# Queries and keys of a head rotated together on GpSimd, and projected three heads ahead

## The chip, the cores and the metric

One core of one Trainium2 chip. The metric is the device time of one execution in microseconds (us), the median of several runs.

## The reference

A token embedding with a layer norm (8 sequences of 512 tokens, 64 channels), one attention layer of 16 heads, and a mixture of 8 experts of which two are taken per token. What bears on this case is the attention's queries and keys. Of each head's 96 query and key channels, 64 are rotated by the position (rotary embedding):

```python
def _rope(x, cos, sin):
    T = x.shape[-2]
    c = cos[:T][None, None]
    s = sin[:T][None, None]
    xr, xi = jnp.split(x, 2, -1)
    return jnp.concatenate([xr * c - xi * s, xr * s + xi * c], -1)
...
cq = _rms(x @ Wcq, q_norm_w)
qn = (cq @ Wq_nope).reshape(B, T, N_HEAD, NOPE).transpose(0, 2, 1, 3)
qr = _rope((cq @ Wq_rope).reshape(B, T, N_HEAD, ROPE).transpose(0, 2, 1, 3), cos, sin)
q = jnp.concatenate([qn, qr], -1)
```

Three attentions share the queries (over a compressed cache, over 128 selected tokens, over a window of 128), and a gate weighs their sum. The keys of the selected tokens and of the window are projected per head and rotated in the same way.

## The kernel before

The five engines run programs of their own, written out by hand, and meet through semaphores. After a setup (embedding, norms, shared latents) comes a loop over 8 batches, in each 16 heads, and in the end the experts. A head has four tiles of 128 query rows. For each tile TensorE does the scores (`scores`, L1340), VectorE adds masks and takes maxima (`maxima`, L1008), ScalarE the exponentials (`probs`, L635), TensorE turns the probabilities into PT (`turn_probs`, L1373 and L1380), ScalarE and VectorE store them as a high and a low half (`take_hi`, L647; `take_lo`, L1018), and TensorE multiplies them with the values (`values`, L1395). VectorE ends a head in `combine`: a reciprocal, the product `coef` of two small SBUF tiles (L1027) and the weighted branches (L1030). One such round is a **turn**. In a turn's step `t` TensorE does the scores of tile `t + 3`, the transposes of tile `t + 1` and the values of tile `t`, so that from `t = 1` on the scores are those of the next head. All engines keep this order.

The queries and keys of a head come earlier. TensorE projects them into the PSUM tile X, which holds one projection at a time (`k_proj`, L1300: ten products; `q_proj`, L1290: twelve). ScalarE copies X to SBUF (`evac_k`, `evac_q`, L576), GpSimd rotates (`rope`, L421 to L429: two products with the tables, L424 and L425, two sums of half rows, L428 and L429) and splits the result into two fp16 halves (`split_key`, L457 and L460; `split_query`, L446 and L449), and SyncE turns these by a transposing DMA into `kh` and `qh` (`turn_keys`, L319; `turn_queries`, L328). `qs` and `kk` have two buffers each, for heads of even and odd number. In turn `h` (L1400 on TensorE, L658 on ScalarE) the projections are those of head `h + 2`: the key's at `t = 0`, the query's at `t = 1`, ahead of that step's scores; the copies stand at the same steps of ScalarE ahead of `take_hi`, and `high_values`, a copy of the values, at `t = 2`. The first two heads of a batch are projected by `lead`, in the last two turns of the batch before. GpSimd's order for a head (`prepare`, L525) is key rotation, key split, query rotation, query split, `low_values` (L480), and then `branch_sum` (L473, L475) of an earlier head. In the last batch GpSimd also normalises rows for the experts (`normalise`, L488) in every second head. The change of batch is `behind` on TensorE, ScalarE and VectorE: the last values, the output's transposes and projection, the next batch's first scores.

## Time and profile before

| what | us |
|---|---|
| median of 3 runs | 1845.62 |
| lowest and highest run | 1845.43, 1846.01 |
| the profiled execution | 1848.94 |
| its span | 1847.0 |
| TensorE busy in it | 1430.7 |
| VectorE busy | 1437.1 |
| ScalarE busy | 1222.9 |
| GpSimd busy | 1434.9 |

The span runs from the first instruction to the last of one profiled execution. Names in the rows: PE is TensorE, DVE VectorE, ACT ScalarE, POOL GpSimd, SP SyncE; L425 is line 425 of the kernel; `big` is the buffer that holds the probabilities, their turned halves and GpSimd's rotation products.

### The profile page before, as it was taken

What the parts mean: (1) busy time and instruction counts of PE and PEld (TensorE: products, weight loads), DVE (VectorE), ACT (ScalarE), POOL (GpSimd) and SP (SyncE); (2) the same over time, 40 slices, a digit from 0 to 9 for tenths busy, and PEclk for the clock granted to TensorE, in tenths of its full rate; (3) what the DMA queues carried; (4) which work ended last, traced back from release to release, by engine and by line L of the source; (5) the groups of instructions that cost most, each with busy time, mean ns of one, the idle gap of its engine ahead of it and who ended that gap; (6) DMA issues with size and microseconds to landing.
All of it is one profiled execution on the core that took longest, in us unless ns stands there. A gap on an engine that the chain in (4) does not pass through costs nothing.

```text
span 1847.0 us, 64237 instructions
## 1 busy us (share of the span) xinstructions
PE 1430.7 (77%) x19368; PEld 1152.9 (62%) x19368; DVE 1437.1 (78%) x4982; ACT 1222.9 (66%) x3280; POOL 1434.9 (78%) x2126
## 2 busy tenths in 40 slices
PE   1041488888888888888888888888888888888778
PEld 0021377767776777777777767677767776766643
DVE  5737588877888788878887888788878887878845
ACT  0041378767777777768776777687768776767634
POOL 6775489877887798779887998698868887889710
PEclk9985699999999999999999999999999999999989
DMA  5110232313222322222222222222222221333200
GB/s 92 22 26 2 47 63 51 58 38 65 54 54 41 65 53 51 44 61 52 58 50 55 53 55 51 54 51 55 55 50 55 51 57 38 55 64 68 53 4 21
DMA packets 327554, 92.04 MB, mean 50 GB/s; under 512 B 321104, under 2 KB 323024, under 8 KB 327520
## 3 DMA queue, kind: packets, MB, share of 16 engines
q1 hardware_dynamic: 324448, 88.48, 24.3%
q0 software_dynamic: 3072, 3.15, 1.0%
q8 instruction: 15, 0.25, 0.1%
q14 instruction: 19, 0.16, 0.0%
HBM read 6.51 MB, written 1.05 MB: 4 GB/s over the span
## 4 chain that ended last, share of the span: by engine, by line
POOL 58%; issue 20%; DVE 8%; PE 7%; POOLq 3%; DMA 2%; ACT 1%; DVEq 0%; ACTq 0%; SPq 0%
POOL big L425 10%; POOL big L424 8%; POOL kparts L460 6%; POOL big L394 5%; POOL vh L480 4%; POOL kparts L457 4%; POOL qparts L446 4%; POOL kk L428 3%; POOL kk L429 3%; POOL qs L428 3%; POOL qs L429 3%; POOL osum L473 2%; DVE S L1008 2%; DMA qh<-qparts 1%; DVE big L1018 1%
## 5 line engine op out<-in xcount | busy, mean ns | idle before, releaser
L635 ACT ACTIVATE big<-S,negm 128x128 f32<-128x128 f32 (+3 forms) x1536 | 575.9, 448 | 209.3 <-DVE negm L1008 208.9
L647 ACT ACTIVATE big<-PT 128x384 f16<-128x384 f32 (+3 forms) x1024 | 426.7, 454 | 133.0 <-PE PT L1373 98.4
L1018 DVE SCALAR_TENSOR_TENSOR big<-PT,big 128x384 f16<-128x384 f32 (+3 forms) x1024 | 472.1, 500 | 32.5 <-ACT big L647 18.7
L1008 DVE CUSTOM_DVE_ANT_0 S<-S,mask_c,unscale 128x128 f32<-128x128 f32 (+3 forms) x512 | 285.0, 557 | 179.4 <-PE S L1348 167.5
L1348 PE MATMUL S<-k1T,qh 128*128 128x128 f16 (+3 forms) x1536 | 298.6, 304 | 117.2 <-DMA qh<-qparts 107.9
L1348 PE MATMUL S<-kh,qh 128*128 128x128 f16 (+1 forms) x3072 | 324.5, 243 | 0.0
L1395 PEld LDWEIGHTS O<-vh,big 128*128 128x128 f16 x8064 | 274.0, 96 | 46.0 <-DVE big L1030 28.5
L1395 PE MATMUL O<-vh,big 128*128 128x33 f16 x8064 | 283.7, 178 | 19.6 <-DVE big L1030 16.3
L1348 PEld LDWEIGHTS S<-kh,qh 128*128 128x128 f16 x3072 | 231.2, 100 | 56.9 <-issue 1.4
L1380 PE MATMUL PT<-cst,big 128*128 128x128 f32 x1408 | 249.3, 282 | 18.8 <-DVE big L1018 16.1
L1373 PE MATMUL PT<-cst,big 128*128 128x128 f32 x1280 | 233.6, 282 | 18.6 <-DVE big L1018 18.2
L1008 DVE CUSTOM_DVE_ANT_0 S<-S,cst,kfix 128x256 f32<-128x256 f32 (+1 forms) x512 | 232.4, 454 | 0.0
L1008 DVE DVE_READ_ACCUMULATOR2_ANT negm<- 128x1 f32 x1536 | 216.6, 141 | 0.2
L1348 PEld LDWEIGHTS S<-k1T,qh 128*128 128x128 f16 x1536 | 110.4, 98 | 165.3 <-issue 124.3
L1380 PEld LDWEIGHTS PT<-cst,big 128*128 128x128 f32 x1408 | 163.0, 144 | 52.2 <-issue 45.4
L1008 DVE CUSTOM_DVE_ANT_0 S<-S,mask_c,kfix 128x128 f32<-128x128 f32 x512 | 181.3, 354 | 0.0
L1373 PEld LDWEIGHTS PT<-cst,big 128*128 128x128 f32 x1280 | 152.3, 144 | 38.4 <-DVE big L1018 25.5
L449 POOL TENSOR_TENSOR qparts<-qs,qparts 128x512 f16<-128x512 f32 x128 | 148.2, 1158 | 18.6
L424 POOL TENSOR_TENSOR big<-kk,cst 128x320 f32<-128x320 f32 x128 | 110.1, 860 | 59.0 <-ACT kk L576 58.8
L460 POOL TENSOR_TENSOR kparts<-kk,kparts 128x480 f16<-128x480 f32 x128 | 140.8, 1100 | 18.6
L1295 PE MATMUL X<-wqh,cqT 128*128 (+1 forms) x1536 | 117.1, 224 | 17.2 <-DVE cqT L960 15.9
L424 POOL TENSOR_TENSOR big<-qs,cst 128x256 f32<-128x256 f32 x128 | 93.6, 731 | 33.3 <-ACT qs L576 33.3
(295 smaller groups left out, 2395.5 us busy)
## 6 DMA issues: line engine op xcount, KB each, us to landing
lat_b<-lat_all SPq DMA_DIRECT2D x8, 448.0 KB, 3.1
qh<-qparts SPq DMA_TRANSPOSE x128, 3.0
kh<-kparts SPq DMA_TRANSPOSE x128, 3.3
xnT_all<-xnT_b SPq DMA_DIRECT2D x14, 128.0 KB, 2.5
xn_b<-xn_all SPq DMA_DIRECT2D x8, 128.0 KB, 2.8
xnT_b<-xnT_all SPq DMA_DIRECT2D x8, 128.0 KB, 2.3
out_dram<-h_all SPq DMA_DIRECT2D x8, 128.0 KB, 2.0
xn_all<-xn_b SPq DMA_DIRECT2D x7, 128.0 KB, 2.0
```

The source lines that it names most:

```text
L424: g.tensor_tensor(tmp[:, 0, 0:tiles, :], v, cos5[:, 0:tiles, :], ALU.mult)
L425: g.tensor_tensor(tmp[:, 1, 0:tiles, :], v, sin5[:, 0:tiles, :], ALU.mult).then_inc(part, 1)
L449: g.tensor_tensor(qparts[:, 1], qs[par][:], qparts[:, 0], ALU.subtract).then_inc(s["q_split"], 1)
L460: g.tensor_tensor(kparts[:, 1, :, NOPE:P], kk[par][:, :, NOPE:P], kparts[:, 0, :, NOPE:P], ALU.subtract).then_inc(s["k_split"], 1)
L635: last = nc.scalar.activation(pr[par][:, lo:lo + n], S[par][:, lo:lo + n], ACT.Exp, bias=negm[par][:, k:k + 1], scale=-1.0)
L647: last = nc.scalar.activation(pT[par][:, 0, lo:lo + n], PT[:, lo:lo + n], ACT.Copy, scale=PSCALE)
L1008: last = v.tensor_tensor_reduce(out=z, in0=z, in1=m, scale=unscale[:] if k == 0 else kfix[:], scalar=3.0e38, op0=ALU.add, op1=ALU.min, acc ...
L1018: v.scalar_tensor_tensor(pT[par][:, 1, lo:lo + n], PT[:, lo:lo + n], PSCALE, pT[par][:, 0, lo:lo + n], ALU.mult, ALU.subtract).then_inc(s[ ...
L1348: last = mm(z[:, lo:lo + n], qh[par][:, c, t * P:(t + 1) * P], keys[:, a, :], start=(c + a == 0), stop=(c == 1))
L1373: last = tp(PT[:, lo:lo + P], src[:, lo:lo + P], ident)
L1380: last = tp(PT[:, lo:lo + P], src[:, lo:lo + P], ident)
L1395: last = mm(o, w[:, c, blocks[i] * P:(blocks[i] + 1) * P], vh[p][:, a, v0 + i, :], start=(j == 0), stop=(j == len(parts) - 1))
```

## The change

`qs` and `kk` of a parity become one buffer `qk` of nine tiles of 128 columns, four of the query and five of the key. For all heads but the first two of a batch one rotation of four instructions runs over the nine tiles; the tables are cosine in nine tiles (longer constants, loaded at the start) and a nine-tile copy of the sine that GpSimd makes in `big` at the start. The splits follow, the key's first. GpSimd's order for a head becomes `low_values`, `branch_sum`, row normalisation (last batch, every second head), rotation, splits (`cycle`). Turn `h` projects head `h + 3` instead of `h + 2`: the key's at `t = 2`, the query's at `t = 3`; ScalarE's copies move along, and `high_values` to `t = 1`. Head 2 of a batch is projected by two more `lead` steps, its query in the last turn of the batch before, its key in `behind`; the turns of heads 13 to 15 project nothing for their own batch. The first two heads keep separate rotations.

```diff
-        qs = [sb(f"qs{i}", [P, NT, QW]) for i in range(2)]
-        kk = [sb(f"kk{i}", [P, 5, P]) for i in range(2)]
+        qk = [sb(f"qk{i}", [P, NT + 5, P]) for i in range(2)]
+        qs, kk = [q[:, 0:NT] for q in qk], [q[:, NT:NT + 5] for q in qk]
         work = big[:].rearrange("p a n -> p (a n)")
-        NPR, NRT, NOB = 7 * P, 2 * 5 * ROPE, NT * 3 * VD
+        NPR, NRT, NOB = 7 * P, 2 * 9 * ROPE, NT * 3 * VD
         pr = [work[:, i * NPR:(i + 1) * NPR] for i in range(2)]
         pT = [work[:, (2 + i) * NPR:(3 + i) * NPR].bitcast(fp16).rearrange("p (c n) -> p c n", c=2) for i in range(2)]
-        rt = [work[:, 4 * NPR + i * NRT:4 * NPR + (i + 1) * NRT].rearrange("p (a t r) -> p a t r", a=2, t=5)
-              for i in range(2)]
-        obr = [work[:, 4 * NPR + 2 * NRT + i * NOB:4 * NPR + 2 * NRT + (i + 1) * NOB].rearrange("p (t k d) -> p t k d", t=NT, k=3)
+        rt9 = work[:, 4 * NPR:4 * NPR + NRT].rearrange("p (a t r) -> p a t r", a=2, t=9)
+        rt = [work[:, 4 * NPR:4 * NPR + 8 * ROPE].rearrange("p (a t r) -> p a t r", a=2, t=NT),
+              work[:, 4 * NPR + 8 * ROPE:4 * NPR + NRT].rearrange("p (a t r) -> p a t r", a=2, t=5)]
+        obr = [work[:, 4 * NPR + NRT + i * NOB:4 * NPR + NRT + (i + 1) * NOB].rearrange("p (t k d) -> p t k d", t=NT, k=3)
                for i in range(2)]
+        sin9 = work[:, 4 * NPR + NRT + 2 * NOB:4 * NPR + NRT + 2 * NOB + 9 * ROPE].rearrange("p (t r) -> p t r", t=9)
...
-        LEAD = ["cq", "qp0", "sel", "k1", "kp0", "qp1", "kp1"]
-        NX = (NH - 2) * 2 + len(LEAD)
+        LEAD = ["cq", "qp0", "sel", "k1", "kp0", "qp1", "kp1", "qp2", "kp2"]
+        NX = (NH - 3) * 2 + len(LEAD)
...
-            def rope(src, tmp, part, done, tiles, n):
-                v = src[:, 0:tiles, NOPE:HD]
-                g.tensor_tensor(tmp[:, 0, 0:tiles, :], v, cos5[:, 0:tiles, :], ALU.mult)
-                g.tensor_tensor(tmp[:, 1, 0:tiles, :], v, sin5[:, 0:tiles, :], ALU.mult).then_inc(part, 1)
-                g.wait_ge(part, n)
-                hf = ROPE // 2
-                g.tensor_tensor(src[:, 0:tiles, NOPE:NOPE + hf], tmp[:, 0, 0:tiles, 0:hf], tmp[:, 1, 0:tiles, hf:ROPE], ALU.subtract)
-                g.tensor_tensor(src[:, 0:tiles, NOPE + hf:HD], tmp[:, 0, 0:tiles, hf:ROPE], tmp[:, 1, 0:tiles, 0:hf], ALU.add).then_inc(done, 1)
+            g.tensor_copy(sin9[:, 0:NT], sin5[:, 0:NT]).then_inc(s["sin_ready"], 1)
+            g.tensor_copy(sin9[:, NT:NT + 5], sin5).then_inc(s["sin_ready"], 1)
+            def rope_count(b, hh, kind):
+                if kind is None:
+                    return b * (NH + 2) + hh + 3
+                return b * (NH + 2) + hh * 2 + ["q", "k"].index(kind) + 1
+            def rope(src, tmp, cos, sin, n):
+                v, hf = src[:, :, NOPE:HD], ROPE // 2
+                g.tensor_tensor(tmp[:, 0], v, cos, ALU.mult)
+                g.tensor_tensor(tmp[:, 1], v, sin, ALU.mult).then_inc(s["rope_t"], 1)
+                g.wait_ge(s["rope_t"], n)
+                g.tensor_tensor(src[:, :, NOPE:NOPE + hf], tmp[:, 0, :, 0:hf], tmp[:, 1, :, hf:ROPE], ALU.subtract)
+                g.tensor_tensor(src[:, :, NOPE + hf:HD], tmp[:, 0, :, hf:ROPE], tmp[:, 1, :, 0:hf], ALU.add).then_inc(s["rope"], 1)
...
-            def split_query(par, b, hh):
+                rope(kk[par], rt[1], cos5, sin5, rope_count(b, hh, "k"))
+            def split_query(par, b, hh, turned):
                 H = b * NH + hh
-                g.wait_ge(s["rope_q"], H + 1)
+                g.wait_ge(s["rope"], turned)
                 g.nop(nofuse=True)
...
-            def prepare(b, h, hh, par, rows=None):
+            def prepare(par, b, hh, x):
+                n = rope_count(b, hh, None)
+                g.wait_ge(s["x_evac"], x + 2)
+                rope(qk[par], rt9, cos9, sin9, n)
+                split_key(par, b, hh, n)
+                split_query(par, b, hh, n)
+            def cycle(b, h, par, rows=None, add=True):
                 x = xbase(b) + h * 2
-                key(par, b, hh, x + x_index(0, "kp"))
-                query(par, b, hh, x + x_index(0, "qp"))
+                low_values(par, b, h + 1)
+                if add:
+                    branch_sum(par, b, h - 1)
                 if rows is not None:
                     normalise(rows, xn_b[:])
-                low_values(1 - par, b, hh - 1)
+                prepare(par, b, h + 3, x + x_index(0, "qp"))
             def heads(b, rows=False):
-                prepare(b, 0, 2, 0, 0 if rows else None)
+                prepare(0, b, 2, xbase(b) + x_lead("kp2"))
+                cycle(b, 0, 1, 0 if rows else None, add=False)
                 with g.Fori(0, NH // 2 - 2) as hp:
-                    prepare(b, hp * 2 + 1, hp * 2 + 3, 1)
-                    branch_sum(0, b, hp * 2)
-                    prepare(b, hp * 2 + 2, hp * 2 + 4, 0, hp + 1 if rows else None)
-                    branch_sum(1, b, hp * 2 + 1)
-                prepare(b, NH - 3, NH - 1, 1)
+                    cycle(b, hp * 2 + 1, 0)
+                    cycle(b, hp * 2 + 2, 1, hp + 1 if rows else None)
+                low_values(0, b, NH - 2)
                 branch_sum(0, b, NH - 4)
                 branch_sum(1, b, NH - 3)
...
-                    if t == 0 and last < 1:
-                        evac_k(p, xb + x_index(0, "kp"), H + 1)
-                    if t == 1 and last < 1:
-                        evac_q(p, xb + x_index(0, "qp"), H + 1)
-                    if t == 2 and last < 2:
+                    if t == 1 and last < 2:
                         high_values(1 - p, b, h + 1)
+                    if t == 2 and xb is not None:
+                        evac_k(1 - p, xb + x_index(0, "kp"), H + 2)
+                    if t == 3 and xb is not None:
+                        evac_q(1 - p, xb + x_index(0, "qp"), H + 2)
...
                     attended(0)
                 probs(0, 0, b, U)
+                if first:
+                    lead(LEAD.index("qp2"), nxt, b * NH)
+                lead(LEAD.index("kp2"), nxt, b * NH)
                 if not first:
                     attended(2)
                 probs(1, 1, b, U + 1)
                 take_hi(0, 0, U)
                 probs(2, 2, b, U + 2)
...
-                with act.Fori(0, NH // 2 - 1) as hp:
+                with act.Fori(0, NH // 2 - 2) as hp:
                     for p in range(2):
                         turn(b, hp * 2 + p, xbase(b) + hp * 4 + p * 2, p, 0, rows=hp if rows and p == 1 else None)
+                turn(b, NH - 4, xbase(b) + (NH - 4) * 2, 0, 0)
+                turn(b, NH - 3, None, 1, 0, rows=NH // 2 - 2 if rows else None)
             def last_heads(b, nxt):
...
-                    if last < 1 and t == 0:
-                        k_proj(h + 2, xb + x_index(0, "kp"))
-                    if last < 1 and t == 1:
-                        q_proj(h + 2, xb + x_index(0, "qp"))
+                    if xb is not None and t == 2:
+                        k_proj(h + 3, xb + x_index(0, "kp"))
+                    if xb is not None and t == 3:
+                        q_proj(h + 3, xb + x_index(0, "qp"))
...
                 pe.wait_ge(s["q_turned"], H * 16 + 32)
                 scores(0, 0, 0, H * NT)
+                if first:
+                    lead("qp2", b, nxt)
+                lead("kp2", b, nxt)
                 if not first:
                     attended(2)
                     attended(3)
...
-                with pe.Fori(0, NH // 2 - 1) as hp:
+                with pe.Fori(0, NH // 2 - 2) as hp:
                     for p in range(2):
                         turn(hp * 2 + p, b * NH + hp * 2 + p, xbase(b) + hp * 4 + p * 2, p, 0,
                              rows=hp if rows and p == 1 else None)
+                turn(NH - 4, b * NH + NH - 4, xbase(b) + (NH - 4) * 2, 0, 0)
+                turn(NH - 3, b * NH + NH - 3, None, 1, 0, rows=NH // 2 - 2 if rows else None)
```

TensorE, a turn's third step from its values on, and the fourth step. X is the projections' tile, S the scores', PT the turned probabilities', O the values' sum. Before:

```order
L1395 MATMUL O<-vh,big 128x33 x18
L1342 REGISTER_ALU
L1348 MATMUL S<-k1T,qh 128x384 x3
L1348 MATMUL S<-kh,qh 128x128 x3
L1348 MATMUL S<-kh,qh 128x256 x3
L1356 ISA
L1373 MATMUL PT<-cst,big 128x128
L1375 REGISTER_ALU
L1380 MATMUL PT<-cst,big 128x128 x2
L1384 REGISTER_ALU
L1395 MATMUL O<-vh,big 128x33 x21
```

The change, the same stretch:

```order
L1421 MATMUL O<-vh,big 128x33 x18
L1314 REGISTER_ALU
L1321 ISA
L1321 MATMUL X<-wqh,cqT 128x128
L1321 ISA
L1321 MATMUL X<-wqh,cqT 128x128 x11
L1368 REGISTER_ALU
L1374 MATMUL S<-k1T,qh 128x384 x3
L1374 MATMUL S<-kh,qh 128x128 x3
L1374 MATMUL S<-kh,qh 128x256 x3
L1382 ISA
L1399 MATMUL PT<-cst,big 128x128
```

The twelve products of the query's projection (`wqh`) now stand between the third tile's values and the scores over 384 columns (the next head's third tile).

ScalarE, the exponentials of the next head's second tile (out of S, 256 columns) and what follows. `qk<-X` is the copy of a projection. Before:

```order
L635 ACTIVATE big<-S,negm 128x256
L635 ACTIVATE big<-S,negm 128x128
L635 ACTIVATE big<-S,negm 128x256
L645 REGISTER_ALU
L647 ACTIVATE big<-PT 128x128
L645 REGISTER_ALU
L647 ACTIVATE big<-PT 128x256
L632 REGISTER_ALU
L633 ISA
```

The change:

```order
L656 ACTIVATE big<-S,negm 128x256
L656 ACTIVATE big<-S,negm 128x128
L656 ACTIVATE big<-S,negm 128x256
L632 REGISTER_ALU
L597 ACTIVATE qk<-X 128x512
L666 REGISTER_ALU
L668 ACTIVATE big<-PT 128x128
L666 REGISTER_ALU
L668 ACTIVATE big<-PT 128x256
L653 REGISTER_ALU
```

The copy of the query now stands behind these exponentials and ahead of the first tile's high halves (out of PT).

GpSimd, one head in the loop over heads, from the key's rotation on. Before:

```order
L424 TENSOR_TENSOR big<-kk,cst 128x320
L425 TENSOR_TENSOR big<-kk,cst 128x320
L426 ISA
L428 TENSOR_TENSOR kk<-big 128x5x32
L429 TENSOR_TENSOR kk<-big 128x5x32
L455 ISA
L457 CAST kparts<-kk 128x5x96
L460 TENSOR_TENSOR kparts<-kk,kparts 128x5x96
L433 REGISTER_ALU
L424 TENSOR_TENSOR big<-qs,cst 128x256
L425 TENSOR_TENSOR big<-qs,cst 128x256
L428 TENSOR_TENSOR qs<-big 128x4x32
```

The change, from the rotation on (`low_values` and `branch_sum` stand ahead of it):

```order
L437 TENSOR_TENSOR big<-qk,cst 128x576
L438 TENSOR_TENSOR big<-qk,big 128x576
L439 ISA
L440 TENSOR_TENSOR qk<-big 128x9x32
L441 TENSOR_TENSOR qk<-big 128x9x32
L467 ISA
L469 CAST kparts<-qk 128x5x96
L470 REGISTER_ALU
L472 TENSOR_TENSOR kparts<-qk,kparts 128x5x96
L458 CAST qparts<-qk 128x512
L461 TENSOR_TENSOR qparts<-qk,qparts 128x512
L490 ISA
```

Four instructions over nine tiles replace four over five and four over four tiles, and the key's split waits for the rotation of both.

## Rows read from the trace of the kernel before

**Rows 1.** The page: busy time of each engine; the chain that ended last.
```profile
PE 1430.7 (77%) x19368; PEld 1152.9 (62%) x19368; DVE 1437.1 (78%) x4982; ACT 1222.9 (66%) x3280; POOL 1434.9 (78%) x2126
...
POOL 58%; issue 20%; DVE 8%; PE 7%; POOLq 3%; DMA 2%; ACT 1%; DVEq 0%; ACTq 0%; SPq 0%
```

**Rows 2.** Timeline of GpSimd, mid-batch: start, duration, operation [idle before <- released by].
```profile
837.95 0.86 POOL L424 TENSOR_TENSOR big<-kk,cst 128x320 f32<-128x320 f32 x1
...
840.98 0.58 POOL L457 CAST kparts<-kk 128x480 f16<-128x480 f32 x1 [0.27 <-POOL kk L429]
...
845.32 0.61 POOL L446 CAST qparts<-qs 128x512 f16<-128x512 f32 x1 [0.19 <-POOL qs L429]
...
848.92 0.86 POOL L424 TENSOR_TENSOR big<-kk,cst 128x320 f32<-128x320 f32 x1
```

**Rows 3.** Waits from 826.94 to 958: who <- for whom: us in total, times, longest.
```profile
PE S L1348 <- DMA qh<-qparts: 15.7, 12, 1.3
...
DVE S L1008 <- PE S L1348: 14.7, 12, 1.4
```

**Rows 4.** Timeline of VectorE, end of the batch's first turn and its second.
```profile
814.86 0.17 DVE L1027 TENSOR_TENSOR coef<-rinv,gate_all 128x12 f32<-128x12 f32 x1
...
815.15 0.56 DVE L1030 TENSOR_TENSOR big<-O,coef 128x384 f32<-128x384 f32 x1
...
815.63 0.75 DVE L1008 CUSTOM_DVE_ANT_0 S<-S,mask_c,unscale 128x512 f32<-128x512 f32 x1
...
819.45 1.02 DVE L1018 SCALAR_TENSOR_TENSOR big<-PT,big 128x384 f16<-128x384 f32 x2 [0.46 <-ACT big L647]
...
822.72 0.63 DVE L1008 CUSTOM_DVE_ANT_0 S<-S,mask_c,unscale 128x384 f32<-128x384 f32 x1
...
824.73 0.55 DVE L1027 TENSOR_TENSOR coef<-rinv,gate_all 128x12 f32<-128x12 f32 x1
...
825.40 0.56 DVE L1030 TENSOR_TENSOR big<-O,coef 128x384 f32<-128x384 f32 x1
...
826.17 0.76 DVE L1008 CUSTOM_DVE_ANT_0 S<-S,mask_c,unscale 128x512 f32<-128x512 f32 x1 [0.21 <-issue]
```

**Rows 5.** Timeline of VectorE, last batch: `combine`'s product of the first and fourteenth head.
```profile
1583.02 0.56 DVE L1030 TENSOR_TENSOR big<-O,coef 128x384 f32<-128x384 f32 x1
...
1740.30 0.56 DVE L1030 TENSOR_TENSOR big<-O,coef 128x384 f32<-128x384 f32 x1
```

**Rows 6.** Groups of GpSimd by line and shape: shapes, count | busy us, mean ns | idle.
```profile
L424 POOL TENSOR_TENSOR big<-kk,cst 128x320 f32<-128x320 f32 x128 | 110.1, 860 | 59.0 <-ACT kk L576 58.8
...
L424 POOL TENSOR_TENSOR big<-qs,cst 128x256 f32<-128x256 f32 x128 | 93.6, 731 | 33.3 <-ACT qs L576 33.3
...
L429 POOL TENSOR_TENSOR kk<-big 128x160 f32<-128x160 f32 x128 | 70.2, 549 | 0.0
...
L429 POOL TENSOR_TENSOR qs<-big 128x128 f32<-128x128 f32 x128 | 58.3, 456 | 0.0
```

**Rows 7.** Timeline of TensorE, the second turn.
```profile
816.15 0.91 PE L1295 MATMUL X<-wqh,cqT 128*128 x12
...
821.43 0.65 PE L1348 MATMUL S<-k1T,qh 128*128 128x384 f16 x3
...
821.91 0.66 PE L1348 MATMUL S<-kh,qh 128*128 128x128 f16 x6
```

**Rows 8.** Timeline of ScalarE, the second turn.
```profile
818.43 0.61 ACT L576 ACTIVATE qs<-X 128x512 f32<-128x512 f32 x1
...
821.72 1.09 ACT L635 ACTIVATE big<-S,negm 128x256 f32<-128x256 f32 x3
```

**Rows 9.** Timeline of GpSimd, the second turn.
```profile
824.10 1.16 POOL L449 TENSOR_TENSOR qparts<-qs,qparts 128x512 f16<-128x512 f32 x1
```

**Rows 10.** Timeline of VectorE, `combine`'s product of the batch's last two heads.
```profile
971.32 0.56 DVE L1030 TENSOR_TENSOR big<-O,coef 128x384 f32<-128x384 f32 x1
...
980.97 0.56 DVE L1030 TENSOR_TENSOR big<-O,coef 128x384 f32<-128x384 f32 x1
```

More of the change, by code:

```diff
@@ L21 @@
 PSCALE = 2.0 ** 15
-K_ID, K_MASK, K_COS, K_SIN, K_IOTA, K_DESC, K_STK, K_END = 0, 128, 384, 704, 1024, 1152, 1164, 1228
+K_ID, K_MASK, K_COS, K_SIN, K_IOTA, K_DESC, K_STK, K_END = 0, 128, 384, 960, 1280, 1408, 1420, 1484
 ARGS = ["x", "L0_tok_token_emb", "L0_tok_instr_emb", "L0_tok_arg_emb", "L0_tok_gamma", "L0_tok_beta",
@@ L51, in tower @@
         ident = cst[:, K_ID:K_ID + P]
-        cos5 = cst[:, K_COS:K_COS + 5 * ROPE].rearrange("p (t r) -> p t r", t=5)
+        cos9 = cst[:, K_COS:K_COS + 9 * ROPE].rearrange("p (t r) -> p t r", t=9)
+        cos5 = cos9[:, 0:5]
         sin5 = cst[:, K_SIN:K_SIN + 5 * ROPE].rearrange("p (t r) -> p t r", t=5)
@@ L205, in tower @@
             "coef_chain", "osum_part", "osum_done",
-            "x_ready", "x_evac", "rope_tq", "rope_tk", "rope_q", "rope_k",
+            "x_ready", "x_evac", "sin_ready", "rope_t", "rope",
             "oT_psum", "oT_act", "oT_dve", "attn_psum", "h_done",
@@ L431, in rope_q @@
             def rope_q(par, b, hh, x):
                 g.wait_ge(s["x_evac"], x + 2)
-                rope(qs[par], rt[0], s["rope_tq"], s["rope_q"], NT, b * NH + hh + 1)
+                rope(qs[par], rt[0], cos5[:, 0:NT], sin5[:, 0:NT], rope_count(b, hh, "q"))
             def rope_k(par, b, hh, x):
                 g.wait_ge(s["x_evac"], x + 2)
-                rope(kk[par], rt[1], s["rope_tk"], s["rope_k"], 5, b * NH + hh + 1)
-            def split_query(par, b, hh):
+                rope(kk[par], rt[1], cos5, sin5, rope_count(b, hh, "k"))
@@ L449, in split_query, with split_key @@
                 g.tensor_tensor(qparts[:, 1], qs[par][:], qparts[:, 0], ALU.subtract).then_inc(s["q_split"], 1)
-            def split_key(par, b, hh):
+            def split_key(par, b, hh, turned):
                 H = b * NH + hh
-                g.wait_ge(s["rope_k"], H + 1)
+                g.wait_ge(s["rope"], turned)
                 g.nop(nofuse=True)
@@ L463, in query @@
                 rope_q(par, b, hh, x)
-                split_query(par, b, hh)
+                split_query(par, b, hh, rope_count(b, hh, "q"))
             def key(par, b, hh, x):
                 rope_k(par, b, hh, x)
-                split_key(par, b, hh)
+                split_key(par, b, hh, rope_count(b, hh, "k"))
             def branch_sum(par, b, hh):
@@ L480, in low_values @@
                 g.tensor_tensor(vh[par][:, 1, :, 0:VD], vall[:, :, ds(hh * VD, VD)], vh[par][:, 0, :, 0:VD], ALU.subtract).then_inc(s["v_split"], 1)
+            g.wait_ge(s["sin_ready"], 2)
             query(0, 0, 0, xbase(0) + x_lead("qp0"))
@@ L706, in lead @@
                 elif kind[:2] == "qp":
-                    evac_q(int(kind[2]), x, H)
+                    evac_q(int(kind[2]) % 2, x, H if kind != "qp2" else H + 1)
                 elif kind[:2] == "kp":
-                    evac_k(int(kind[2]), x, H)
+                    evac_k(int(kind[2]) % 2, x, H if kind != "kp2" else H + 1)
             def behind(b, nxt, U, first):
@@ L729, in behind @@
                 probs(2, 2, b, U + 2)
-            for i in range(len(LEAD)):
+            for i in range(LEAD.index("qp2")):
                 lead(i, 0)
@@ L1517, in _ @@
             last.then_inc(s["rank_psum"], 1)
-            for kind in LEAD[2:]:
+            for kind in LEAD[2:LEAD.index("qp2")]:
                 lead(kind, 0, 0)
@@ L1659, in _constants @@
     ang = np.outer(np.arange(T, dtype=np.float32), f)
-    for col, tab in ((K_COS, np.cos(ang)), (K_SIN, np.sin(ang))):
-        for t in range(5):
+    for col, tab, n in ((K_COS, np.cos(ang), 9), (K_SIN, np.sin(ang), 5)):
+        for t in range(n):
             rows = tab[(t % NT) * P:(t % NT) * P + P]
```

## The prediction

> **What bounds the kernel now.** I read the page first: GpSimd is busy for 78% of the span, no more than VectorE and hardly more than TensorE, but the chain that ended last runs through GpSimd for 58% of the span [rows 1]. Shares don't say where, so the next view is GpSimd's own order of time. In the middle of a batch one head takes it from the key's first product at 837.95 to the next head's at 848.92, 10.97 us, and the only idle time in between is the short wait for its own result ahead of each split (0.27 and 0.19 us) [rows 2]. Nobody else releases it: it is the bound there. The waits of that stretch show who pays. In twelve heads TensorE waits 15.7 us for the turned queries to land, and VectorE 14.7 us for the scores behind them, 1.2 to 1.3 us a head [rows 3].
>
> How fast could a head go if GpSimd were quicker? One turn per batch answers that: the second, for which GpSimd had worked ahead during the change of batch. Between the two products of `combine`, 815.15 and 825.40, it takes 10.25 us [rows 4]. So even a free GpSimd would buy 0.7 us a head in the present order of the other engines, and the question is whether that order stays as good. A batch has that turn and twelve of 10.97, 141.9 us in all; seven batches are like it, and the last, with the rows normalised on GpSimd too, takes 157.28 us for its thirteen turns, 1583.02 to 1740.30 [rows 5].
>
> **The rotation.** Four instructions take the place of eight. A product over four tiles of 64 takes 731 ns, over five 860 [rows 6]: 129 ns a tile, so nine tiles come to 1376. A sum over four half tiles takes 456, over five 549. Nine lie between 456 + 5 x 65 = 0.78 (half the products' slope, for half the columns) and 456 + 5 x 93 = 0.92; I take 0.82, nearer the slope that has the longer rows behind it. New: 2 x 1.38 + 2 x 0.82 = 4.40. Old: 2 x 0.86 + 2 x 0.73 + 2 x 0.55 + 2 x 0.46 = 5.20. With 0.19 for the second wait ahead of a split, which is gone since both halves are turned before the first split, GpSimd saves 0.8 + 0.19, about 1.0 us a head. Its head would take 10.0. In the fourteen heads of a batch that are turned in this way that would be 14 us, if GpSimd remained the bound.
>
> **What the projections' move costs.** The key's projection goes from a turn's first tile to its third, the query's from the second to the fourth; there TensorE now does the query's twelve products ahead of the scores of the next head's third tile. I walk the free turn of 10.25 with that edit, in us behind `combine`'s product at 815.15 [rows 4, 7, 8]:
> - VectorE's second half of the probabilities (third tile) starts at 819.45, 4.30 behind. It waited 0.46 for ScalarE, whose query copy stood in front; a shorter copy of the values stands there now, which I count as nothing (0 to 0.1).
> - TensorE turns that tile, does its values and starts the scores in question at 821.43, 1.98 later. VectorE takes them up at 822.72, just when they land (821.91 + 0.66 + 0.15): there is no slack. The query's twelve products take 0.91 and now stand in front, so VectorE gets them 0.91 later, and idles for that long.
> - From there to the start of `coef` are 2.01 (822.72 to 824.73), and `combine`'s product follows 0.12 behind `coef`'s end. Bare, `coef` takes 0.17 (at 814.86). Sum: 4.30 + 1.98 + 0.91 + 1.29 + 2.01 + 0.17 + 0.12 = 10.78.
>
> The key's ten products stand in front of the second tile's scores, where TensorE would wait for VectorE anyway; I count nothing (0 to 0.4). In every second turn VectorE goes around its loop: the maxima start 0.77 behind `combine`'s product at 825.40, and only 0.48 behind the one at 815.15, so 0.29 comes on top of one turn in two; while GpSimd was late this was hidden [rows 4]. The mean of this path is 10.92.
>
> **What the rotation does to VectorE.** `coef` took 0.55 in the free turn, not 0.17, and ended at 825.28; GpSimd's split of the queries, which was running when it came, ended at 825.26 [rows 4, 9]. VectorE's product of two SBUF tiles waited for GpSimd's instruction to end. The Trainium skill states it as a rule (SBUF — State Buffer, Who interferes with whom): a VectorE instruction with two SBUF inputs and a GpSimd instruction that reads SBUF use one shared port pair, and the later one is blocked until the first is done. Here it speaks against longer instructions on GpSimd, and the trace agrees by 0.02 us.
>
> When does the rotation run now? It needs the query's copy, and ScalarE does that last, behind the exponentials of the second tile, which end at 821.72 + 1.09, 7.66 behind `combine`; the copy takes 0.61 [rows 8], so the rotation begins at about 8.3. Its first product runs to 9.6, its second to 8.3 + 1.33 + 1.38 = 11.0. `coef` comes at 10.5, into the middle of the second product, and must wait until 11.0; `combine`'s product starts at 11.13. This path holds in every turn, because the copy is itself set by the turn: it is a loop that closes on itself, and GpSimd, done with a head after 10.0, waits for the copy each time. With the 0.29 in one turn of two the mean is 11.27, against 10.97 now. **So the expected gain is not collected: GpSimd ceases to be the bound, and the turn becomes longer by itself.**
>
> The price of a product of nine tiles decides this. The Trainium skill gives about 2.6 cycles at 1.2 GHz an element for GpSimd's two-input operations (GPSIMD Engine Reference, Elementwise — side-by-side cycle accounting), so an estimate from that page is 1.25 us for 576 elements where my rows give 1.38; by it the turn would be 0.26 shorter, 11.01 in the mean, and the kernel would stand about 22 us lower than my sum. The same rate makes 0.55 of four tiles, for which the row has 0.73, so I keep the rows.
>
> **The sum.** A batch has twelve turns with projections from the second on, and then one without. For that one I take 9.9, between the free turn's 10.25 and the batch's last, 971.32 to 980.97, 9.65 [rows 10]. 12 x 11.27 + 9.9 = 145.1, against 141.9: +3.2. Of the change of batch: the first turn grows as the second does (+0.9), the third head's key projection comes on top in `behind` (+0.5) and goes from the first turn's head (-0.5); its query projection falls into the last turn, where GpSimd is late with its own sums; I take +0.8, between 0 and 1.4. Per batch +4.0, seven batches +28.
>
> The last batch: 157.28 in thirteen turns is 24.2 a pair. GpSimd saves 1.97 of it, 22.2; the turn's own path gives 2 x 11.27 = 22.5 and now decides, with some row work: 11.35 a turn. 12 x 11.35 + 9.9 = 146.1, -11.2; the normalisation now stands ahead of the first rotation, so I take -9.
>
> The start: GpSimd's two copies of the sine table stand in its wait for the first query copy, and the longer constants (256 columns more) land ahead of work that waits for other things; nothing, at most 1. Total +28 - 9 = +19. The profiled execution took 1848.94 (span 1847.0), so its like would take 1868; the median of the runs, 1845.62, lies 3.3 under it, and **I predict 1864.6 for the median, 1% slower.** About 0.2%, 3.7 us, is what a measurement of this kernel can tell from no change.
>
> **The rivals.**
> - *GpSimd stays the bound, faster by 5%.* If VectorE and TensorE have more slack than I read, a turn takes 10.0: 13 x 10.0 is 11.9 a batch less, 83 in seven, and some 13 in the last: 1750. For it speaks the idle 1.2 us a head [rows 3]; against it the free turn, where GpSimd held nobody and which still took 10.25 [rows 4]. Chance 0.09.
> - *The port is not hit.* If the rotation starts half a microsecond earlier or `coef` comes 0.6 later, `coef` falls between products and the path of 10.78, 10.92 in the mean, decides: 12 x 10.92 + 9.9 + 0.8 = 141.7, nothing per batch; the last batch gives 11: 1834. It decides from the point at which the copy of the query ends before 7.7 instead of 8.3. Chance 0.17.
> - *A new wait on the landing.* The rotation starts at 8.3; even if the query's split came a whole GpSimd head of 10.0 later, at 18.3, the scores need it two turns on, at about 25. That leaves the transposing DMA 6 to 7 us, and TensorE has waited for it 1.3 at the longest [rows 3], so against; but if the nine-tile products take over 1.6 (no row shows the slope beyond five tiles), `coef` waits 0.5 longer, turns take 11.7, and the kernel 1895. Chance 0.08.
> - *It moves and nets out.* The path of 11.0 to 11.1 with a good last batch lies within 0.2%: chance 0.07.
>
> My forecast has what is left, 0.59. Slower by over 0.2%: 0.59 and 0.08, 0.67; faster 0.26; same 0.07. The range takes the forecast with its terms at their ends (a turn of 11.1 to 11.5, 1850 to 1885) and the case of the missed port down to 1825: it leaves out GpSimd as bound, the low end of the missed port and the late landing. The forecast's own range is 1850 to 1885.
>
> **What would show it.** Right: GpSimd's products over 576 elements at about 1.38, its idle time of 1 us or so ahead of the first one put down to ScalarE's copy, every turn; no more wait of TensorE for the turned queries; VectorE's wait for scores at the next head's third tile, 0.6 to 0.9 in each turn; `coef` at 0.5 to 0.8, ending with GpSimd's second product; turns alternating by 0.3. Wrong: `combine` at even 10.0 us with GpSimd without idle time, or a `coef` of 0.17. If the third-tile wait is missing, my walk of TensorE is at fault; if `coef` is short, the start of the rotation.

## The result: 1939.41 us, 5.1% slower, and the profile after

The changed kernel takes 1939.41 us in the median of four runs (1936.72 to 1941.68), against 1845.53: a ratio of 1.051, interval 1.049 to 1.053. The forecast was slower, but 1864.6, and its range ended at 1885. The profiled execution took 1940.28, its span 1938.4. Some executions on the chips of the experiments below, the kernel before among them, took some 40 us more than the others of the same kernel; they are left out of the times and ratios given here.

The page of the changed kernel: busy time of each engine, and the queue that loads instructions (packets, MB, share).

```profile
PE 1486.7 (77%) x19368; PEld 1190.4 (61%) x19368; DVE 1472.6 (76%) x4982; ACT 1205.7 (62%) x3280; POOL 1360.8 (70%) x1680
...
q8 instruction: 79, 1.29, 0.3%
```

GpSimd is busy for 70% instead of 78%, so the rotation did become cheaper, and nobody else became fuller: VectorE 76%, TensorE 77% [rows 1]. TensorE's busy time grew from 1430.7 to 1486.7 with exactly as many products, which means that some ran slower. And the instruction queue moved 79 packets; on the page of the kernel before that line reads:

```profile
q8 instruction: 15, 0.25, 0.1%
```

GpSimd's rotation by line and shape:

```profile
L437 POOL TENSOR_TENSOR big<-qk,cst 128x576 f32<-128x576 f32 x112 | 157.6, 1407 | 178.8 <-ACT qk L597 178.6 <-POOL pairsel L583 0.2
...
L438 POOL TENSOR_TENSOR big<-qk,big 128x576 f32<-128x576 f32 x112 | 157.5, 1406 | 0.0
...
L441 POOL TENSOR_TENSOR qk<-big 128x288 f32<-128x288 f32 x112 | 88.9, 794 | 0.0
```

The prices are those of the forecast: 1.41 a product (1.38), 0.79 a sum (0.82). The idle time ahead of the first product is 1.6 us a head (178.8 over 112), all but 0.2 of it put down to ScalarE's copy: GpSimd waits for the copy now and is no longer the bound.

A turn in mid-batch, VectorE, GpSimd and ScalarE, answering to [rows 4, 8, 9]:

```profile
874.47 0.56 DVE L1056 TENSOR_TENSOR big<-O,coef 128x384 f32<-128x384 f32 x1
...
882.85 0.63 DVE L1034 CUSTOM_DVE_ANT_0 S<-S,mask_c,unscale 128x384 f32<-128x384 f32 x1 [0.68 <-PE S L1374]
...
884.97 0.75 DVE L1053 TENSOR_TENSOR coef<-rinv,gate_all 128x12 f32<-128x12 f32 x1
...
885.84 0.56 DVE L1056 TENSOR_TENSOR big<-O,coef 128x384 f32<-128x384 f32 x1
...
898.30 0.56 DVE L1056 TENSOR_TENSOR big<-O,coef 128x384 f32<-128x384 f32 x1
```

```profile
882.92 1.41 POOL L437 TENSOR_TENSOR big<-qk,cst 128x576 f32<-128x576 f32 x1 [1.28 <-ACT qk L597]
...
884.28 1.41 POOL L438 TENSOR_TENSOR big<-qk,big 128x576 f32<-128x576 f32 x1
```

```profile
882.23 0.61 ACT L597 ACTIVATE qk<-X 128x512 f32<-128x512 f32 x1
```

From `combine`'s product at 874.47 to the next at 885.84 it is 11.37, the forecast's longer turn (11.42). The steps are there too: the copy of the query ends at 882.84, 8.4 behind; the rotation starts at 8.45, its second product ends at 885.69; `coef`, which came at 884.97, ends at 885.72. VectorE waits 0.68 for the scores behind the query's products. But the next turn, 885.84 to 898.30, takes 12.46, where 11.13 was forecast. Stretches of these two turns (busy time of TensorE, its weight loads, VectorE, ScalarE and GpSimd, then the granted clock):

```profile
874.50:885.80 11.30, 9.33 (x142) 7.70 (x142) 9.60 (x35) 8.40 (x24) 9.18 (x12) 1.00 0.27 52
...
885.80:898.30 12.50, 10.75 (x142) 9.07 (x142) 9.78 (x36) 8.64 (x25) 9.27 (x12) 0.86 0.25 47
...
885.00:888.60 3.60, 1.83 (x24) 1.22 (x23) 3.48 (x11) 1.86 (x6) 3.10 (x5) 1.00 0.00 0
...
889.20:892.20 3.00, 3.00 (x37) 2.69 (x35) 1.23 (x4) 2.37 (x8) 2.85 (x5) 0.50 0.49 94
...
873.60:877.20 3.60, 1.65 (x24) 1.16 (x22) 3.27 (x10) 1.58 (x5) 3.10 (x5) 1.00 0.00 0
```

The third row is the stretch around `combine` ahead of the second turn, the fourth lies inside that turn, and the last is the stretch around `combine` ahead of the first turn. In the first turn the granted clock is 1.00, in the second 0.86, and within it there are 3 us at 0.50, that is at 1.2 GHz instead of 2.4, with TensorE busy all the time. Ahead of the fall stand 3.6 us, around `combine`, in which it was busy for 1.83.

### The profile page after: what moved, and what is told of

Its sections match the earlier page's. It is cut to its first block and busy times, and to the rows that moved or that the text cites. A ratio compares the mean times of both kernels' runs of the same rounds, so it can differ in the third digit from the quotient of the medians.

```text
span 1938.4 us, 63686 instructions
## 1 busy us (share of the span) xinstructions
PE 1486.7 (77%) x19368; PEld 1190.4 (61%) x19368; DVE 1472.6 (76%) x4982; ACT 1205.7 (62%) x3280; POOL 1360.8 (70%) x1680
## 5 line engine op out<-in xcount | busy, mean ns | idle before, releaser
L1374 PE MATMUL S<-k1T,qh 128*128 128x128 f16 (+3 forms) x1536 | 314.5, 317 | 32.9 <-issue 29.8
L437 POOL TENSOR_TENSOR big<-qk,cst 128x576 f32<-128x576 f32 (+2 forms) x144 | 183.2, 1272 | 221.3 <-ACT qk L597 221.1
L1374 PE MATMUL S<-kh,qh 128*128 128x128 f16 (+1 forms) x3072 | 338.0, 249 | 0.0
L1399 PE MATMUL PT<-cst,big 128*128 128x128 f32 x1280 | 243.4, 291 | 90.7 <-DVE big L1044 90.6
L1374 PEld LDWEIGHTS S<-kh,qh 128*128 128x128 f16 x3072 | 241.5, 103 | 63.5 <-issue 3.3
L1406 PE MATMUL PT<-cst,big 128*128 128x128 f32 x1408 | 261.3, 292 | 3.4 <-DVE big L1044 2.5
L1399 PEld LDWEIGHTS PT<-cst,big 128*128 128x128 f32 x1280 | 157.2, 148 | 124.1 <-DVE big L1044 105.6
L1406 PEld LDWEIGHTS PT<-cst,big 128*128 128x128 f32 x1408 | 168.3, 149 | 43.4 <-issue 29.7
L597 ACT ACTIVATE qk<-X 128x480 f32<-128x480 f32 (+1 forms) x256 | 156.6, 612 | 21.2 <-PE X L1321 17.4
L461 POOL TENSOR_TENSOR qparts<-qk,qparts 128x512 f16<-128x512 f32 x128 | 148.2, 1158 | 18.6
L438 POOL TENSOR_TENSOR big<-qk,big 128x576 f32<-128x576 f32 x112 | 157.5, 1406 | 0.0
L472 POOL TENSOR_TENSOR kparts<-qk,kparts 128x480 f16<-128x480 f32 x128 | 140.5, 1098 | 18.6
```

Of the source, the lines that this page charges most:

```text
L437: g.tensor_tensor(tmp[:, 0], v, cos, ALU.mult)
L438: g.tensor_tensor(tmp[:, 1], v, sin, ALU.mult).then_inc(s["rope_t"], 1)
L461: g.tensor_tensor(qparts[:, 1], qs[par][:], qparts[:, 0], ALU.subtract).then_inc(s["q_split"], 1)
L597: return nc.scalar.activation(dst, src, ACT.Copy)
L1374: last = mm(z[:, lo:lo + n], qh[par][:, c, t * P:(t + 1) * P], keys[:, a, :], start=(c + a == 0), stop=(c == 1))
L1399: last = tp(PT[:, lo:lo + P], src[:, lo:lo + P], ident)
```

## Where the time went

Sums from the starts of `combine`'s product in the profiled executions, in us: the thirteen turns between the first fourteen heads of a batch and the last two turns, each over seven batches; the seven changes of batch; the last batch's thirteen turns.

| kernel | 13 turns x 7 | last two x 7 | 7 changes | last batch | span |
|---|---|---|---|---|---|
| before | 999.5 | 167.1 | 176.6 | 157.3 | 1847.0 |
| after | 1071.4 | 173.2 | 202.6 | 147.8 | 1938.4 |
| e_warm | 1016.6 | 173.3 | 212.7 | 146.7 | 1895.4 |
| e_loop7 | 1076.6 | 173.3 | 174.9 | 147.4 | 1916.8 |
| e_warm7 | 1015.3 | 173.2 | 180.6 | 147.4 | 1861.8 |
| e_coefp | 964.1 | 173.4 | 197.0 | 146.3 | 1825.1 |
| e_back | 949.0 | 173.3 | 208.2 | 146.7 | 1823.2 |
| e_best | 953.5 | 173.3 | 180.5 | 145.4 | 1797.4 |
| e_best_sep | 955.3 | 173.6 | 179.6 | 156.6 | 1811.0 |
| e_best_hv0 | 923.0 | 172.1 | 171.4 | 145.5 | 1754.9 |

The last batch gave back 9.5, as forecast (9). The loss stands in the thirteen turns, +72 where +22 was forecast, and in the changes of batch with the two turns ahead of them, +32 where +6 was. In the thirteen turns of seven batches the granted clock falls in 46 of 91: 41 of them take over 12 us, and the other five are last turns of the thirteen, without a projection, which take 10.7 instead of 9.7. In the kernel before it falls in 10, which take 12.0 to 12.1.

The change of batch has a stretch of its own. TensorE, the output's projection and the next batch's first instruction, and VectorE's sum behind the former:

```profile
1046.72 3.76 PE L1518 MATMUL O<-wproj,oT 128*128 128x64 f32 x32
...
1055.62 1.46 PE L1374 MATMUL S<-k1T,qh 128*128 128x512 f16 x3 [5.15 <-issue]
```

```profile
1050.63 0.42 DVE L1170 TENSOR_TENSOR h_all<-O,h_all 128x256 f32 x1 [2.00 <-PE O L1518]
```

TensorE leaves its loop over batches as soon as VectorE has taken the sum over (`h_done`, 1051.05), and jumps back to its start. The next matmul comes at 1055.62, 4.6 later, and the trace names nothing that it waited for. The row it starts with takes 1.46 where the same scores take 0.82 at full clock: the clock has fallen again. The stretch of that row, and the queue that loads instructions from 1050 to 1054 and from 1054 to 1058:

```profile
1054.00:1057.00 3.00, 1.38 (x5) 0.56 (x6) 0.00 (x0) 0.00 (x0) 1.49 (x2) 0.50 0.03 7
```

```profile
q8 instruction: 1, 0.02, 2.4%
...
q8 instruction: 1, 0.02, 1.8%
```

From one batch's first `combine` to the next, 862.0 to 1068.8, that queue moves ten packets; in the kernel before it moves none from 815.2 to 1006.2.

## The experiments

**e_warm: TensorE kept busy where the projections used to be.**

```diff
+                    if xb is not None and t == 0:
+                        k_proj(h + 3, xb + x_index(0, "kp"), False)
+                    if xb is not None and t == 1:
+                        q_proj(h + 3, xb + x_index(0, "kp"), False)
                     if xb is not None and t == 2:
```

The last argument leaves out the signal that the products are there.

> The change as it is, but TensorE does the key's ten and the query's twelve products once more, for nothing, at the places they had before (first and second step of a turn, into X, which is free there). Theory A (the clock): at full clock the turn is what was forecast, 11.07 and 11.37 in alternation, and the turns of 12.4 and the long change of batch come from TensorE's granted clock, which falls where TensorE has little to do at a turn's start. Then the granted clock stays 1.00 in mid-batch, no turn is over 11.6, and the kernel takes about 1885 to 1895 although it does more. Rival B (the clock falls because turns are long, or 12.4 has another cause): every second turn stays at 12.4 and the kernel at 1940 or above.

1894.8, ratio to before 1.022 (1.019 to 1.025). Two turns, and the stretch around `combine`:

```profile
1046.00:1057.10 11.10, 10.10 (x162) 8.73 (x163) 9.67 (x35) 8.40 (x23) 9.28 (x12) 1.00 0.38 55
...
1057.10:1068.40 11.30, 10.76 (x169) 9.06 (x166) 9.64 (x35) 8.84 (x24) 9.21 (x11) 1.00 0.27 52
...
1056.30:1059.90 3.60, 3.13 (x44) 2.62 (x43) 3.27 (x10) 1.73 (x5) 3.10 (x5) 1.00 0.00 0
```

With 22 more products a turn the kernel is 45 us faster. In these turns the clock stays at 1.00, the stretch around `combine` has 3.13 busy of 3.60, no turn is over 12, and turns are 11.07 and 11.38: theory A. The clock still falls in six of the 91 turns, and all six are the last of a batch's thirteen, which projects nothing and so got no spare products. The long change of batch stays, so it is not part of this.

**e_key0: only the key's projection and copy back at the first step.** (`t == 2` becomes `t == 0` for both.)

> Only the key's projection and copy go back to the first step; the query's stay in the fourth. Theory A: the key's products fill the gap, the clock stays up in most turns, and the query's copy is as late as before, so turns are 11.1 and 11.4 and the kernel takes 1880 to 1895. Rival B: the query's copy alone sets the turn and the clock with it; 12.4 in every second turn, within 1% of 1940.

1888.2, ratio 1.019 (1.015 to 1.023). The time is theory A's: ten useful products at the turn's start are worth as much as e_warm's spare ones. This rests on the time alone.

**e_back: both back,** key at `t == 0`, query at `t == 1`.

> Key back in the first step and query in the second, copies with them, still three heads ahead and rotated together. Theory A with the walk of the prediction: the query's products no longer stand ahead of the third tile's scores, the rotation starts some 4 us earlier and coef no longer meets its second product; full clock; turns of 10.3 to 10.7, kernel 1780 to 1805, faster than both. Rival C (the nine-tile rotation itself costs, wherever it starts): turns of 11.0 or more, kernel at 1846 or above.

Its profiled execution took 1825.1 and one more 1823.4, beside 1851.1 for the kernel before in the same job, some 1.4% faster, without an interval. Turns are 10.24 and 10.76, about as expected (10.3 to 10.7), and at full clock; the kernel missed the expected 1780 to 1805, because the change of batch stayed at 30 (208.2 in the table, against 180.5 in e_best). Rival C falls: with joint rotation turns are under 11.0.

**e_coefp: `coef` reads its reciprocals from PSUM.**

```diff
-                v.reciprocal(rinv[:].rearrange("p t k -> p (t k)").unsqueeze(2), o3[:, :, VD:VD + 1]).then_inc(s["coef_chain"], 1)
+                v.reciprocal(o3[:, :, VD:VD + 1], o3[:, :, VD:VD + 1]).then_inc(s["coef_chain"], 1)
...
-                v.tensor_tensor(coef[:], rinv[:], bc(gate_all[:, ds(b, 1), :], [P, NT, 3]), ALU.mult).then_inc(s["coef_chain"], 1)
+                v.tensor_tensor(coef[:], den, bc(gate_all[:, ds(b, 1), :], [P, NT, 3]), ALU.mult).then_inc(s["coef_chain"], 1)
```

`den` is the view of O's columns of sums, in PSUM.

> The change, with the reciprocal of the sums left in PSUM, so that coef reads one SBUF tile instead of two. Theory A: coef takes 0.2 instead of 0.55 to 0.83, turns at full clock get 0.3 shorter (10.78 and 11.07), the falls of the clock stay; kernel about 1905 to 1915. Rival (coef's wait is not on the path, or it is not two SBUF inputs that make it wait): coef still ends with GpSimd's second product, or the time stays within 0.3% of 1939.

1830.4, ratio 0.990 (0.986 to 0.993): 109 us off the changed kernel, and faster than the kernel before, by one operand of a product of twelve columns. The group of `coef` in the changed kernel, and here:

```profile
L1053 DVE TENSOR_TENSOR coef<-rinv,gate_all 128x12 f32<-128x12 f32 x128 | 90.6, 708 | 10.5
```

```profile
L1054 DVE TENSOR_TENSOR coef<-O,gate_all 128x12 f32<-128x12 f32 x128 | 21.9, 171 | 10.5
```

The mechanism is the one expected: with one operand in PSUM `coef` doesn't wait for GpSimd, 171 ns against 708 in the mean. The size was not. Turns are 10.40 and 10.80, 0.6 shorter rather than 0.3, and the clock falls in 4 turns instead of 46. TensorE's pause around `combine` shrank with `coef`'s wait; this is the stretch around the one at 835.08, with 2.40 where the changed kernel had 1.83 and 1.65:

```profile
834.50:838.10 3.60, 2.40 (x29) 1.62 (x27) 3.33 (x14) 2.43 (x8) 3.12 (x4) 1.00 0.00 0
```

Of the 107 us that the turns gave back, some 55 are the 0.6 in 91 turns; the rest goes to the clock, by subtraction. That the shorter pause is what kept the clock up is argued from these rows and e_warm, not tried apart. The Trainium skill (SBUF — State Buffer, Who interferes with whom) has a VectorE instruction with at most one SBUF input, outside its two-port modes, free of GpSimd. The two rows of `coef` agree.

**e_bcoef: the same edit on the kernel before.**

> The kernel before, with coef's reciprocal left in PSUM. Theory A: GpSimd is the bound there, so the turns in mid-batch stay at 10.97; only the batch's second turn, the last two and the last batch may get some tenths shorter: within 0.4% of 1846. Rival (coef's wait held the kernel before too): turns under 10.7 and more than 1.5% faster.

1847.2, ratio 0.999 (0.996 to 1.002). `coef` got shorter here too, and nothing followed, except in the batch's second turn, which was free of GpSimd (9.88 instead of 10.25). That is what is to be expected where GpSimd is the bound.

**e_loop7: the written-out turns back into the loop, on TensorE and ScalarE.**

```diff
-                with pe.Fori(0, NH // 2 - 2) as hp:
+                with pe.Fori(0, NH // 2 - 1) as hp:
                     for p in range(2):
                         turn(hp * 2 + p, b * NH + hp * 2 + p, xbase(b) + hp * 4 + p * 2, p, 0,
                              rows=hp if rows and p == 1 else None)
-                turn(NH - 4, b * NH + NH - 4, xbase(b) + (NH - 4) * 2, 0, 0)
-                turn(NH - 3, b * NH + NH - 3, None, 1, 0, rows=NH // 2 - 2 if rows else None)
```

Turn 13 now projects a sixteenth head that nobody uses; so that its weights are read inside a tile, the four weight tiles became parts of one.

> The change, but turns 12 and 13 of a batch run as a seventh pass of the loop over heads on TensorE and ScalarE, as before, instead of being written out behind it (turn 13 then projects a sixteenth head that nobody uses). Theory D (code): TensorE's batch loop is short again, so its jump back needs no loading of code; the instruction queue's packets fall from 79 to about 15, TensorE's wait with no releaser at a batch's first turn falls from 5 to about 1 us, the change of batch from 29.6 to about 25, six times: kernel about 1910. The turns of 12.4 stay. Rival E (the projections and the first joint rotation at the change of batch cost the time): it stays at 29 or more and the kernel at 1939.

1917.0, ratio 1.038 (1.035 to 1.041). Its instruction queue, and TensorE's first matmul of a batch:

```profile
q8 instruction: 15, 0.25, 0.1%
```

```profile
1043.40 0.82 PE L1374 MATMUL S<-k1T,qh 128*128 128x512 f16 x3 [1.37 <-DVE h_all L1170]
```

TensorE is idle for 1.37 and starts 0.8 behind the end of VectorE's sum (1042.61), which the trace now names as its releaser; the seven changes take 174.9 instead of 202.6. Turns still reach 12.5, as expected; turn 13 with its useless projection grew by 1 us, which is why the kernel gained 22 and not 28.

**e_unroll: the kernel before, with TensorE's last pass over two heads written out.**

```diff
-                with pe.Fori(0, NH // 2 - 1) as hp:
+                with pe.Fori(0, NH // 2 - 2) as hp:
...
+                for p in range(2):
+                    h = NH - 4 + p
+                    turn(h, b * NH + h, xbase(b) + h * 2, p, 0, rows=NH // 2 - 2 if rows and p == 1 else None)
```

> The kernel before, with nothing changed but that TensorE's last pass over two heads is written out behind its loop. Theory D: about 79 packets of instructions instead of 15, 4 to 5 us more at six changes of batch, turns as before (10.97): kernel 1867 to 1877. Rival E: the same time as before, within 0.2%.

1878.3, ratio 1.017 (1.012 to 1.021). The instruction queue, and TensorE's waits at key projections that nothing in the trace released (total, times, longest), here and in the kernel before:

```profile
q8 instruction: 80, 1.31, 0.3%
```

```profile
PE X L1304 <- issue: 40.2, 42, 5.5
```

```profile
PE X L1304 <- issue: 19.4, 50, 1.6
```

Nothing else was changed, and six changes of batch went from 25 to 30 us, while the seventh, behind which the loop isn't entered again, stayed at 26.4. That is the code's price by itself. The traces give the length of TensorE's loop over batches: the records of one batch, weight loads and waits included, with the repeated passes of the loop over heads counted once. It is 2090 in this kernel and in the changed one, against 1465 before, 1514 in e_loop7 and 1606 in e_warm7 below. The Trainium skill (Runtime: NRT & Kernel Launch, Instruction fetch mechanics) says that TensorE's instruction memory has 2048 instructions, filled in blocks of 256, and that a taken branch whose target isn't in the window that is held has to wait for a fetch. It gives that window as two blocks. The runs agree with the 2048 as far as they go: 2090 loads code in every batch, and 1606, well over two blocks, doesn't. Where the limit lies between them no run here shows.

**e_warm7: e_warm and e_loop7 together.**

> The change with both of its unforeseen costs taken away together: the spare products that keep TensorE busy at a turn's start, and the seventh pass of the loop over heads. If the two are separate they add: 1939.4 less 44.6 less 22.4 is 1872.4, so 1868 to 1878, turns of 11.07 and 11.37, a change of batch of about 25; what is left over the kernel before is then what the walk of the prediction forecast (1864.6). If they overlap: 1880 or more.

1864.2, ratio 1.009 (1.007 to 1.012). The clock falls in none of the 91 turns. Without these falls and the loading of code the changed kernel takes what the walk had said, 1864.6, though with 22 more products a turn: +16 in the seven batches' turns (forecast +22), +10 around the change of batch (+6), -10 in the last batch (-9). That it comes this near is in part luck, since the first two differences cancel.

**e_best: e_back, e_coefp and e_loop7 together.**

> The change with the projections and copies back at the first and second step, coef's reciprocal in PSUM and seven passes of the loop over heads. If the three causes (clock with placement, port, code) add up: full clock in mid-batch, turns of 10.0 to 10.4, a change of batch of about 25, kernel 1775 to 1800, over 2.5% faster than before. If something else is the bound there (GpSimd's own head of 10.0, or the change of batch): turns at 10.5 or the change of batch at 29, 1805 or more.

1799.2, ratio 0.973 (0.971 to 0.975), at the upper end of what was expected. The gains of e_back and e_loop7 add up; e_coefp's 109 us do not come on top, as turns are 10.21 and 10.79, as in e_back. In e_back `coef` took 0.17 to 0.20 in mid-batch already, so it no longer decides.

**e_best_sep: e_best with key and query rotated apart.**

```diff
-                rope(qk[par], rt9, cos9, sin9, n)
-                split_key(par, b, hh, n)
-                split_query(par, b, hh, n)
+                rope(kk[par], rt[1], cos5, sin5, n + 1)
+                split_key(par, b, hh, n + 1)
+                g.wait_ge(s["x_evac"], x + 2)
+                rope(qs[par], rt[0], cos5[:, 0:NT], sin5[:, 0:NT], n + 2)
+                split_query(par, b, hh, n + 2)
```

> The best version so far (projections back, coef from PSUM, seven passes), but key and query rotated apart, eight instructions, as in the kernel before. If the joint rotation is what makes room: GpSimd's head takes 10.97 again and bounds the turn, 10.9 to 11.0 against 10.2 and 10.8, and the kernel takes 1835 to 1855. Rival (the gain came from the order of the other engines alone): within 0.5% of 1799.

1811.3, ratio 0.980 (0.978 to 0.982): only 12 slower, so neither expectation held. GpSimd's first product of two heads, and `combine`'s products of the same stretch:

```profile
991.88 0.86 POOL L439 TENSOR_TENSOR big<-qk,cst 128x320 f32<-128x320 f32 x1
...
1002.88 0.87 POOL L439 TENSOR_TENSOR big<-qk,cst 128x320 f32<-128x320 f32 x1
```

```profile
986.21 0.56 DVE L1059 TENSOR_TENSOR big<-O,coef 128x384 f32<-128x384 f32 x1
...
996.42 0.56 DVE L1059 TENSOR_TENSOR big<-O,coef 128x384 f32<-128x384 f32 x1
...
1007.21 0.56 DVE L1059 TENSOR_TENSOR big<-O,coef 128x384 f32<-128x384 f32 x1
```

GpSimd's head takes 11.00 again, and the turns 10.2 and 10.8 all the same. With three heads ahead GpSimd may fall behind by half a microsecond a head: in the fourth batch its first product of a head starts 5.8 us ahead of the first `combine` and, twelve heads on, 0.5 behind the thirteenth. That is less than one head, and it catches up at the change of batch. In the last batch, where it has the rows as well, the lead is used up, turns reach 13.6, and most of the loss stands there (156.6 against 145.4). So in mid-batch it isn't the joint rotation that frees the turn from GpSimd but the head start; the new order of GpSimd's work came with it, and no run tells these two apart.

**e_best_hv0 and e_best_hv2: the copy of the values moved.** In e_best VectorE waits 1.06 in every turn for the third tile's high half; the copies of the values and of the query stand in front of it. `high_values` goes to `t == 0` in the one, to `t == 2` in the other.

> The best version with the copy of the values at the first step of ScalarE instead of the second, where it stands with the query's copy in front of the high half that VectorE waits 1.06 for in every turn. If that wait is on the turn's path: 0.3 to 0.45 less a turn, 1760 to 1780. If what follows it has slack, or the second tile's high half gets late in its place: within 0.5% of 1799.

> The best version with the copy of the values at the third step, as in the kernel before. VectorE's wait of 1.06 gets 0.45 shorter, but GpSimd, whose order for a head begins with that copy, starts a head some 2 us later and its rotation moves with it. If GpSimd has the slack (it was busy 9.1 to 9.4 us of a turn): 1770 to 1790; if not, turns of 10.6 to 10.8 in the mean and 1805 to 1825.

1758.2, ratio 0.951 (0.949 to 0.953), and 1760.7, 0.952 (0.950 to 0.955): the two can't be told apart. The row in e_best, and in e_best_hv0:

```profile
845.84 1.02 DVE L1044 SCALAR_TENSOR_TENSOR big<-PT,big 128x384 f16<-128x384 f32 x2 [1.06 <-ACT big L670]
```

```profile
845.61 1.02 DVE L1044 SCALAR_TENSOR_TENSOR big<-PT,big 128x384 f16<-128x384 f32 x2 [0.47 <-ACT big L670]
...
855.94 1.02 DVE L1044 SCALAR_TENSOR_TENSOR big<-PT,big 128x384 f16<-128x384 f32 x2 [0.73 <-ACT big L670]
```

The wait falls to 0.47 and 0.73 in two turns that follow each other, and the turns are 9.88 and 10.45; the change of batch is 24.4. That is the fastest version, 4.9% under the kernel before. In hv2 the wait is 0.73 in every turn, and the turns are the same. Both came out below the better of their two expectations, hv0 by 2 us (1760 to 1780) and hv2 by 9 (1770 to 1790): GpSimd has the slack, as in e_best_sep.

## Why the prediction was right in direction and wrong in size

- **GpSimd ceases to be the bound:** right, with the prices of the rotation, and against the rival by which it stays so. That it was the bound before, e_bcoef bears out.
- **The loop of copy, rotation, `coef` and turn:** right, 11.07 and 11.37 at full clock (forecast 11.13 and 11.42). The wait for the third tile was 0.68 where the walk had 0.91, so the path without GpSimd was too long in the walk: e_coefp, where `coef` doesn't wait, has 10.6 in the mean, not 10.92. That path didn't decide.
- **The last batch:** right, -9.5 for -9, and by its own terms: most turns are 11.32 to 11.40 (forecast 11.35) and the one without a projection 9.99 (9.9).
- **The sum over twelve turns failed by a term it lacked.** "12 x 11.27 + 9.9" took every row from stretches at full clock and asked only whose way the moved products stand in, not what they had done where they stood. There they had kept TensorE busy at the turn's start. Taking them away let the granted clock fall in 46 turns of 91; e_warm, which puts products back there, takes 55 us less in the turns (1071.4 to 1016.6). The trace of the kernel before had a sign of it: its ten turns with the clock at 0.86 are most of why its thirteen turns take 142.8 in the mean (999.5 over 7), where the prediction counted 141.9.
- **"Of the change of batch ... I take +0.8, between 0 and 1.4" failed.** It counted the two lead projections and not the code that was written out. With the two turns ahead of it the change grew by 4.6 a batch; e_loop7 gives 28 us of 32 back, and e_unroll makes them out of nothing else.
- **"The port is not hit", 1834,** did not come about; e_coefp builds that case by another way and takes 1830.4. That is near by luck: turns are 10.6 in the mean and the code still loads, so two errors cancel.
- **The rival of 11.7 a turn** comes by the prediction's own terms to about 1906, not 1895. Nothing hung on it, since the products took 1.41.

What stays open is why the clock falls in about every second turn and not in each: the last of the stretches above, around `combine` of the turn that kept its clock, has TensorE busy for 1.65 of 3.60, less than the 1.83 ahead of a fall.

## What to carry to other kernels

When work is moved off an engine's place in a cycle, ask what that engine does there afterwards: a pause on TensorE can cost its clock, and then a wait of 0.6 us a turn costs twice that (e_coefp). Writing loop passes out is a change of its own; look at the instruction queue's packets on the page before and after. And work started one round further ahead can hide an engine that is slower than the turn for as long as a batch lasts (e_best_sep), and here the head start, with the new order of GpSimd's work, left only 12 us for a faster GpSimd to gain.

## What the runs showed that was not expected

- Extra products made a kernel faster: 45 us (e_warm).
- A product of twelve columns took 0.71 us in the mean with both operands in SBUF while GpSimd worked, and 0.17 with one in PSUM; on the path that was worth 109 us (e_coefp), off it nothing (e_bcoef).
- Two turns written out on TensorE cost 5 us at each jump back of the loop around them, with 65 packets of instructions more in all (e_unroll).
